# Shared last norm, halved first loads, later rows of x and two reordered steps in a cross-attention and FFN kernel

## The reference

```python
def layernorm(x): return (x - mean(x)) / sqrt(var(x) + 1e-5)
# attention: 32 query heads of 128, 4 key/value heads, keys and values of context and latents together
h   = concatenate([ctx, layernorm(x)], axis=1)
q   = layernorm(x) @ Wq;  k = h @ Wk;  v = h @ Wv
x   = x + softmax(q k^T / sqrt(128)) v @ Wo
# FFN: shared part and a low-rank part weighted by the two best of 8 gate logits
n   = layernorm(x)
y   = relu(n @ up)**2 @ down + ((n @ fc1 @ expert) * sum(top2(n @ gate_w))) @ fc2
out = x + layernorm(y) * gamma + beta
```

## Time and profile before

| | |
|---|---|
| median of 3 runs | 1747.38 us (1745.17 to 1749.41) |
| profiled execution | 1745.41 us, its span 1743.6 us |
| PE busy | 1725.9 us (99%) |
| DVE, ACT, POOL busy | 965.0, 692.7, 961.1 us |
| DMA | 296.31 MB, mean 170 GB/s |

### The profile page before, as it was taken

One profiled execution on the slowest core, in us unless ns is written; L12 is line 12 of the kernel. 1 busy time (PEld: TensorE's weight loads), 2 busy tenths in 40 slices (PEclk: granted clock), 3 DMA queues, 4 the chain that ended last, 5 costly groups with the idle time before them and its releaser, 6 DMA issues.

```text
span 1743.6 us, 24837 instructions
## 1 busy us (share of the span) xinstructions
PE 1725.9 (99%) x8613; PEld 1519.3 (87%) x8613; DVE 965.0 (55%) x1495; ACT 692.7 (40%) x1350; POOL 961.1 (55%) x785
## 2 busy tenths in 40 slices
PE   9999999999999999999999999999999999999997
PEld 8888998889999988988988898889888988888886
DVE  3521112634334357875787588667657465555567
ACT  3221212234343357733774377347613233332340
POOL 2546452235555548874867476735534345565557
PEclk9999999999999999999999999999999999999999
DMA  9888886256768668843773477334222312121224
GB/s 276 278 283 270 278 284 223 85 162 212 229 194 275 208 198 294 287 155 129 226 252 109 139 243 225 121 103 142 82 84 85 93 35 73 55 61 48 64 92 147
DMA packets 196567, 296.31 MB, mean 170 GB/s; under 512 B 19216, under 2 KB 158736, under 8 KB 195600
## 3 DMA queue, kind: packets, MB, share of 16 engines
q1 hardware_dynamic: 196496, 295.41, 52.2%
HBM read 197.10 MB, written 98.27 MB: 169 GB/s over the span
## 4 chain that ended last, share of the span: by engine, by line
PE 92%; DMA 3%; DVE 2%; POOL 1%; SPq 1%; issue 1%; ACT 0%; ACTq 0%; POOLq 0%; DVEq 0%
PE bank L1972 29%; PE bank L1973 29%; PE bank L1974 29%; PE bank L2189 5%; DMA tile_region<-in_ctxT 1%; DMA k_ctx_scratch<-small_region 1%; DMA slab_raw<-in_wkv 1%; DMA weight_sums_scratch<-slab_raw 1%; DMA mid_region<-k_latents_scratch 0%; PE bank L2311 0%; DMA small_region_unrounded<-in_slabs 0%; PE bank L2044 0%; POOL act_region L905 0%; POOL slab_raw L916 0%; POOL tile_region L952 0%
## 5 line engine op out<-in xcount | busy, mean ns | idle before, releaser
L952 POOL TENSOR_TENSOR tile_region<-tile_region,small 128x487 f32<-128x487 f32 x224 | 220.9, 1023 | 70.7 <-DVE small L1595 70.7
L1972 PE MATMUL bank<-mid_region 128*128 128x488 f32 (+4 forms) x532 | 219.3, 412 | 1.1 <-DMA mid_region<-k_latents_scratch 0.6
L1974 PE MATMUL bank<-mid_region 128*128 128x488 f32 (+4 forms) x532 | 199.7, 375 | 0.0
L1973 PE MATMUL bank<-mid_region 128*128 128x488 f32 (+4 forms) x496 | 185.9, 375 | 0.0
L1972 PE MATMUL bank<-mid_region,act_region 128*125 128x512 f32 (+3 forms) x448 | 174.8, 390 | 0.1
L1974 PE MATMUL bank<-mid_region,act_region 128*125 128x512 f32 (+3 forms) x448 | 174.4, 389 | 0.0
L1226 ACT ACTIVATE tile_region<-bank,small 128x487 f32<-128x487 f32 x224 | 153.5, 686 | 29.8 <-DVE small L1599 29.8
L1973 PE MATMUL bank<-mid_region,act_region 128*125 128x512 f32 (+3 forms) x418 | 162.9, 390 | 0.0
L936 POOL TENSOR_TENSOR slab_split<-slab_raw,slab_split 128x512 fp32r<-128x512 f32 x64 | 87.3, 1366 | 130.5 <-ACT slab_split L1181 130.5
L1258 ACT ACTIVATE mid_region<-bank 125x512 fp32r<-125x512 f32 x224 | 136.5, 612 | 55.8 <-PE bank L2189 55.8
L1599 DVE TENSOR_REDUCE small<-bank 128x1 f32<-128x487 f32 x224 | 145.9, 652 | 22.5 <-PE bank L1974 22.5
(11 more groups left out here) (243 smaller groups left out, 4336.0 us busy)
## 6 DMA issues: line engine op xcount, KB each, us to landing
slab_raw<-in_slabs SPq DMA_DIRECT2D x112, 256.0 KB, 3.5
q_scratch<-y_region SPq DMA_DIRECT2D x16, 1792.0 KB, 8.1
mid_region<-q_scratch SPq DMA_DIRECT2D x32, 896.0 KB, 6.9
slab_raw<-in_slabs SPq DMA_DIRECT2D x37, 512.0 KB, 3.6
weight_sums_scratch<-slab_raw SPq DMA_DIRECT2D x32, 512.0 KB, 5.0
v_scratch<-slab_split SPq DMA_DIRECT2D x8, 1536.0 KB, 8.0
slab_raw<-weight_sums_scratch SPq DMA_DIRECT2D x48, 256.0 KB, 4.8
mid_region<-v_scratch SPq DMA_DIRECT2D x32, 384.0 KB, 3.2
```

The costliest lines, as they stand in the source:

```text
L952: pool.tensor_tensor(PR[i][:, 0:KEYS], PR[i][:, 0:KEYS], rrow[:, i:i + 1].broadcast_to([P, KEYS]), ALU.mult).then_inc(s_pn, 1)
L1972: pe.matmul(out_ap, w[0], a[0], start=first, stop=False)
L1973: pe.matmul(out_ap, w[0], a[1], start=False, stop=False)
L1974: return pe.matmul(out_ap, w[1], a[0], start=False, stop=last)
```

## The change

Last norm: for tiles 0 to 5 DVE subtracts the mean and multiplies by gamma in one operation that doesn't wait for the deviation, then makes the reciprocal; ACT multiplies the tile by it; POOL adds x and beta. For tile 6 the first product with gamma stands ahead of the reciprocal. First loads: piece 1 and tiles 2 and 3 come in halves too, and both contexts' tiles stand ahead of piece 3's wait. The eight loads of x move from behind the second context to behind the second half of the first pair of query slabs. The high part of the third context moves behind the first two units of batch 1. The beta sum of tile 5 moves behind the low parts of the two fc1 slabs.

```diff
+        def piece_half(s, l):
+            return part(RB, (2 * (s // 2) + l) * PIECE + 512 * (s % 2), 512)
+        def piece_half_raw(s):
+            return PRAW[s // 2][:, 512 * (s % 2):512 * (s % 2) + 512]
...
-            for s in range(2):
-                sp.dma_start(PRAW[0][:, 512 * s:512 * s + 512], wkv[0, :, 512 * s:512 * s + 512]).then_inc(s_half[s], 16)
+            for s in range(4):
+                at = 512 * (s % 2)
+                sp.dma_start(PRAW[s // 2][:, at:at + 512], wkv[s // 2, :, at:at + 512]).then_inc(s_half[s], 16)
                 sp.dma_start(CRAW[:, s, :], ctxT[0, :, s, :]).then_inc(s_fhalf[s], 16)
...
+            sp.dma_start(PRAW[2], wkv[2]).then_inc(s_piece[2], 16)
+            for k in range(2, 4):
+                sp.dma_start(CRAW[:, 2 * k:2 * k + 2, :], ctxT[0, :, 2 * k:2 * k + 2, :]).then_inc(s_first[k], 16)
+            sp.wait_ge(s_plo, 2)
+            sp.dma_start(PRAW[0], wkv[3]).then_inc(s_piece[0], 16)
+            for k in range(4, NK):
+                sp.wait_ge(s_plo, k)
                 sp.dma_start(PRAW[k % 3], wkv[k]).then_inc(s_piece[k % 3], 16)
-            sp.wait_ge(s_flo, 5)
+            sp.wait_ge(s_flo, 6)
             sp.dma_start(CRAW, ctxT[1]).then_inc(s_ctx, 16)
-            for b in range(B):
-                sp.dma_start(X8[0:SQ, b, :], x[b * SQ:(b + 1) * SQ, :]).then_inc(s_x, 16)
...
                         load_piece(2 * b, u)
+                    if first and u == 1:
+                        for i in range(B):
+                            sp.dma_start(X8[0:SQ, i, :], x[i * SQ:(i + 1) * SQ, :]).then_inc(s_x, 16)
...
-                if g[0] == "wo_last" and g[2] == 1:
-                    r = g[1]
+                done = {("wo_last", RT - 1, 0): RT - 2, ("wo_last", RT - 1, 1): RT - 1}
+                r = done.get(g[:3], g[1] if g[0] == "wo_last" and g[2] == 1 and g[1] < RT - 2 else None)
+                if r is not None:
                     pool.wait_ge(s_xn, B + r + 1)
                     pool.tensor_tensor(Y[:, r, :], Y[:, r, :], BETA, ALU.add).then_inc(s_x2b, 1)
...
-            pool.wait_ge(s_gamma, 16)
             for r in range(RT - 1):
-                pool.wait_ge(s_xn, B + RT + r + 1)
-                pool.tensor_tensor(Y[:, r, :], Y[:, r, :], GAMMA, ALU.mult).then_inc(s_gm, 1)
                 pool.wait_ge(s_gm, r + 1)
...
-            ctx_hi(2, 0, N_CTX)
             for u in range(N_CTX):
+                if u == 2:
+                    ctx_hi(2, 0, N_CTX)
                 ctx_unit_hi(1, u)
                 sqrt_var(u, u, SQ)
...
+                if eh == 1 and r < RT - 1:
+                    act.wait_ge(s_xn, B + RT + r + 1)
+                    act.wait_ge(s_rs, r + 1)
+                    act.activation(Y[:, r, :], Y[:, r, :], ACT.Copy, scale=rs[:, r:r + 1]).then_inc(s_gm, 1)
...
                 if eh == 1 and r < RT - 1:
-                    normalise(r, n, Y[:, r, :], Y[:, r, :])
+                    if r == 0:
+                        dve.wait_ge(s_gamma, 16)
+                    dve.scalar_tensor_tensor(out=Y[:, r, :], in0=Y[:, r, :], scalar=mv[:, r, 0:1], in1=GAMMA,
+                                             op0=ALU.subtract, op1=ALU.mult).then_inc(s_xn, 1)
+                    dve.wait_ge(s_sd, n + 1)
+                    dve.reciprocal(rs[:, r:r + 1], sd[:, r:r + 1]).then_inc(s_rs, 1)
...
+            r = RT - 1
+            centred(r, 0)
+            reciprocal_sd(r, B + RT + r)
+            dve.wait_ge(s_xin[r % 3], 16 * (r // 3 + 1))
+            scaled(r, 0)
+            centred(r, 1)
+            scaled(r, 1)
```

More of the change, by code:

```diff
@@ L506, in xattn_ffn @@
         s_x2b = sem("x2_beta")
[L507 removed]
+        s_gm = sem("row_tile_scaled")
+        s_rs = sem("inverse_deviation")
         s_o = sem("out_tile")
@@ L1109, in piece_hi @@
             def piece_hi(k):
-                act.wait_ge(s_piece[k % 3], 16 * (k // 3 + (k % 3 > 0)))
+                act.wait_ge(s_piece[k % 3], 16 * (k // 3 + (k % 3 == 2)))
                 act.activation(piece(k, 0), PRAW[k % 3], ACT.Copy).then_inc(s_phi, 1)
-            for s in range(2):
+            for s in range(4):
                 act.wait_ge(s_half[s], 16)
-                act.activation(part(RB, 512 * s, 512), PRAW[0][:, 512 * s:512 * s + 512], ACT.Copy).then_inc(s_phi, 1)
+                act.activation(piece_half(s, 0), piece_half_raw(s), ACT.Copy).then_inc(s_phi, 1)
                 act.wait_ge(s_fhalf[s], 16)
                 act.activation(HT[0][:, 0, s, 0:SC], CRAW[:, s, :], ACT.Copy).then_inc(s_fhi, 1)
-            for k in range(1, 4):
+            for k in range(2, 4):
                 piece_hi(k)
@@ L1495, in _ @@
             link(dve.memset(small[:, 208:209], EPS))
-            for s in range(2):
+            for s in range(4):
                 dve.wait_ge(s_phi, s + 1)
-                dve.tensor_tensor(part(RB, PIECE + 512 * s, 512), PRAW[0][:, 512 * s:512 * s + 512],
-                                  f32(part(RB, 512 * s, 512)), ALU.subtract).then_inc(s_plo, 1)
+                dve.tensor_tensor(piece_half(s, 1), piece_half_raw(s), f32(piece_half(s, 0)),
+                                  ALU.subtract).then_inc(s_plo, 1)
                 dve.wait_ge(s_fhi, s + 1)
@@ L1503, in _ @@
                                   ALU.subtract).then_inc(s_flo, 1)
-            for k in range(1, NK):
-                dve.wait_ge(s_phi, k + 2)
+            for k in range(2, NK):
+                dve.wait_ge(s_phi, k + 3)
                 dve.tensor_tensor(piece(k, 1), PRAW[k % 3], f32(piece(k, 0)), ALU.subtract).then_inc(s_plo, 1)
@@ L1948, in _, with centred, scaled @@
                 if eh == 1 and r < RT - 1:
-                    normalise(r, n, Y[:, r, :], Y[:, r, :])
[L1952 to L1956, removed]
-                half = Y[:, r, cols_of(eh)]
-                link(dve.scalar_tensor_tensor(out=half, in0=half, scalar=mv[:, r, 0:1], in1=GAMMA[:, cols_of(eh)],
-                                              op0=ALU.subtract, op1=ALU.mult))
+                    if r == 0:
[4 more added lines that the diff above has]
+                    dve.reciprocal(rs[:, r:r + 1], sd[:, r:r + 1]).then_inc(s_rs, 1)
+            def centred(r, eh):
+                half = Y[:, r, cols_of(eh)]
+                chain[0] += 1
+                dve.scalar_tensor_tensor(out=half, in0=half, scalar=mv[:, r, 0:1], in1=GAMMA[:, cols_of(eh)],
+                                         op0=ALU.subtract, op1=ALU.mult).then_inc(s_link, 1)
+            def scaled(r, eh):
+                half = Y[:, r, cols_of(eh)]
+                dve.wait_ge(s_link, chain[0])
                 dve.scalar_tensor_tensor(out=half, in0=half, scalar=rs[:, r:r + 1], in1=XB[r % 3][:, cols_of(eh)],
                                          op0=ALU.mult, op1=ALU.add).then_inc(s_oh, 1)
+            r = RT - 1
[5 more added lines that the diff above has]
+            scaled(r, 1)
         @block.tensor
@@ L2057, in _ @@
                     ctx_step(u, 0, s)
-            for j in range(1, 4):
-                pe.wait_ge(s_plo, j + 2)
-                pe.wait_ge(s_flo, j + 2)
+            for j in range(2, 4):
+                pe.wait_ge(s_plo, j + 3)
+                pe.wait_ge(s_flo, j + 3)
                 for u in range(NKV):
```

21 lines of the change are left out of this document (6 added, 15 removed).

## The result

The changed kernel takes 1750.24 us (median of 14 runs, 1746.33 to 1755.01) against 1745.6 us for the kernel before in the same sessions (14 runs, 1743.35 to 1749.41): a ratio of 1.0028, 95% interval 1.0017 to 1.0038. That is slower by about 0.28%, a little over the 0.2% named in the prediction; the forecast was 1749.4, range 1742.4 to 1752.6. The profiled execution took 1752.76 us, its span is 1751.0; beside 1745.41 and 1743.6 of before that is +7.35 us, so it lies above the median difference.

What follows compares the result with a forecast made beforehand. PE, busy 99% of the span, bounds the kernel. Batch 2 +3.8, clock +2.0, fc1 -1.1 and tail -2.7 give +2.0 on 1745.41, 1747.4; that execution lay 2.0 below the median, so 1749.4 us, range 1742.4 to 1752.6.

Steps and rivals of the forecast that it cites:

- The path: Start of batch 2: x delays the sums' store, then pair 1's load, POOL's sums and context 2's low part, then PE.
- Two signs: Before batch 2: load of pair 1 issued near 62 us, and PE idle 4 to 7 us.
- Rival (a): Sums' store not pushed back, x slipping into gaps or the store passing it; about -5 us, 1742.4; chance 0.25.
- the +3.8 of batch 2: Moved x leaves DMA engines idle, so batch 2 starts at 79.1 instead of 75.34 us; bounds 2 to 5.5.
- The clock: TensorE restarts slowly after standing idle 5.7 us before batch 2; +2.0 us, between 0 and 2.8.
- The row of the start: Kernel start, 1.27 to 6.6 us: matmul starts twice as far apart as later, which cost 2.8 us.
- The row of the tail: Behind the last matmul: granted clock stayed full for 3.7 us, then fell; basis for a restart price of 0.
- First loads: First K products: loading in halves removes a hole of 1.3 us; whether the gain lasts depends on batch 2's start.
- fc1: First fc1 product: POOL's slab low part ahead of the beta sum removes PE's wait; -1.1 us (0.9 to 1.2).
- Tail: Last norm behind PE's last matmul: last operation ends at 1738.5 instead of 1741.17; -2.7 us (2.0 to 2.9).
- Rival (c): Tail gives back 1 us: ACT's scaling ends later, DVE's tile 6 product meets POOL's last sum; +3.0, 1750.4; chance 0.07.
- Rival (b): Batch 2: store 5 us late and full slow stretch of 2.8, if the hole passes 3.7 us; +4.0, 1751.4; chance 0.15.

Runs made afterwards that it cites:

- the kernel with a busy PE: The changed kernel plus 66 unread identity transposes on TensorE behind batch 1 of the context, filling its standstill; 1748.26 us, ratio 1.0017 to the kernel before.
- the kernel with x back: The changed kernel with only the loads of x put back behind the second context; 1738.65 us, ratio 0.9957 to the kernel before.

## Why the prediction was right, and where it wasn't

The time was 0.8 us off, but that is partly luck. Of the difference I had forecast +2.0 us; the ratio says +4.9. The three runs of before that I had, 1747.38, lay 1.8 above the 14 runs' 1745.6, and this hid more than half of the gap. In the profiled execution it is +7.35.

**The path was right at each step**: hole at 10.4 gone, DMA share 0.09 and 0.00 from 26 to 32 us, store landing in 20.3 us behind x, POOL's two steps following (the sums in 6.25 us instead of 6.94), PE idle, a slow stretch, no wait at fc1, tail shorter. Two signs came larger than I had named them: the load of pair 1 went out at 66.16 instead of near 62, and PE stood idle for 9.7 us instead of 4 to 7. Rival (a), the store not pushed back, is out: x has landed at 59.0, the K stores issued behind it at 61.0 and 61.3, context 2 at 64.9, the sums at 66.1, in the order of issue. "DMA: Bandwidth & Descriptors" (the Trainium skill, Queues, rings and completion order) says that completion is not FIFO per issuing engine; these landings show next to nothing of it (the one inversion between 16 and 50 us is the K store of 33.89, which landed at 41.4 behind the slab half issued after it, 41.1). The trace of before shows more: the slab halves issued at 34.17 and 36.15 landed 1.4 and 0.9 us ahead of the K stores issued before them. But no trace has the sums' store passing x.

**The term that was mis-sized is the +3.8 of batch 2.** Here it was +7.18; the load of pair 1 went out 8.15 later. The engines' idle time grew by 5.2 us (0.17 of 40 less 0.05 of 32) where I had 3.8: context 1 landed at 28.1, past my upper bound of 27.8, and the first K store went out at 31.86 instead of 30.4. The other 2.8 us are a term that I hadn't: 33.2 us of busy engines instead of 30.4. Of these, 0.9 are 0.24 MB more that were moved from 26 us on (8.88, 8.64), in part because the engines had begun to run dry before that (share 0.81 from 20 to 26 us, before 0.96); 1.9 are the rate, 267 GB/s while busy instead of 284. I had taken the rate as fixed. It isn't: the kernel with a busy PE, which is the same up to 72 us, had 26.4, 30.6 us and +4.2, nearly my numbers. So the forecast fits one trace and not the other, and the bounds of 2 to 5.5 were too tight, since a spread of landings had no place in them. Whether it is spread alone is open: while busy, the engines moved 267, 275 and 286 GB/s in the three kernels with all of x moved and 279 to 298 in the ten others, so a slower mix of transfers is a rival that no run excludes. The spread of the times doesn't settle it: after's 14 runs span 8.7 us, but the 11 of the kernel with the busy PE only 3.6. And the halves brought the load of pair 1 forward where x stayed, which wasn't in my sum either.

**The clock** was +2.6 (I took 2.0, bound 2.8), confirmed by the filler. The row of the start, half rate, was a good one. The row of the tail, 3.7 us of idle time before the fall, was not a measure for a hole: here the share of 0.69 between 74 and 76 puts the fall at about 74.8, 2 us behind PE's last matmul. And the price follows the hole: the 6.5 us of the kernel with x moved alone cost 1.3. My 2.0 was for a hole of 5.7 us, so that it came near the 2.6 of a hole of 9.7 is luck.

**First loads** -1.3: right, and right that it doesn't last by itself (halves alone 1.0001). PE was even ready for batch 2 1.9 us earlier (72.8, 74.7); 0.4 of it was there before the hole. (The tiles that now stand ahead of piece 3's wait are the last four of the first context, not tiles of both contexts, as the section on the change says.) What I missed is that it becomes a gain once the store is earlier too; in the kernel with x back the whole hole at batch 2 is gone.

**fc1** -1.1: -1.16 in the trace, -1.0 by the ratio alone. **Tail** -2.7: -2.68 in the trace, -2.4 alone. Rival (c), the tail giving back 1 us, didn't come about: ACT's scaling took 1.15, not 1.06, but the 0.4 us of clearance to POOL held, and the product took 0.75. For tiles 3 and 4 it took 1.91 and 1.79 over 1024 columns, beside POOL's sums of 2.4, against 1.28 for tile 5 alone, off the path. SBUF — State Buffer (the Trainium skill, Who interferes with whom) calls the port pair that the two share an exclusive lock, so that the later one waits for the whole of the other; at 1734.49 that gives 0.70 us of waiting (POOL ends at 1735.19) and 1.28 of work, 1.98, and the row says 1.79: nearly so.

**Rival (b)**, store over 5 us late with nearly the full slow stretch, is what the profiled execution shows, though not its condition: a hole over 3.7 us was not enough, as the 6.5 us hole with its 1.3 shows. It had 1751.4; I gave it 0.15, too little next to 0.53, and so a change of 0.28%, just beyond the 0.2% that I named, had a chance of only 0.20.

**Attention** +1.4 in this pair of traces was no term of mine. It also differs between kernels that are alike there: its wait on POOL is 1.4, 2.0, 2.2 and 2.4 us in before, after, norm alone and x back, and the time from the 61st matmul of batch 2 to the transposes ahead of fc1 is 1251.1 to 1253.6 us in the twelve kernels with POOL's old order, 1251.9 in before and 1253.2 in after. So I count it as spread and not as an effect.

## What to carry to other kernels

When a transfer is moved away from a stretch, ask first what else may be issued there: if nothing, its bytes were free where they stood, and the engines' idle time comes back at the next landing that someone waits for, here whole and more (5.2 us more of it in after, 8.15 us at the load). A transfer that fills a forced gap is worth keeping even if nobody needs its data soon; half of it may be enough in most runs. And take a landing time as one value of a spread (26.6 to 27.9 us for context 1 in six traces of kernels alike there), not as a fixed number, above all where a gain at one place only shows once the next hole is closed.

## What the runs showed of the hardware

- Two kernels with the same order of work up to 72 us, one trace each, moved 8.75 MB in 30.6 us and 8.88 MB in 33.2 us of busy DMA engines (286 and 267 GB/s), and the 1.5 MB load of context 1 landed 26.4 and 28.1 us into the span. I had taken both as fixed.
- SP's own issues can slow down while transfers are outstanding: in after, context 2's issue took 2.59 us and the two stores of sums 3.93 (43.19 and 45.82), with 10 or 11 transfers outstanding. Their number alone doesn't decide it: the last loads of x took 0.43 us each with 9 to 11 outstanding.
- A standstill of 9.7 us of PE cost 2.6 us on top of itself through the halved clock, one of 6.5 us 1.3; behind 66 transposes in its place the matmuls ran at full rate at once.
